# Score stage: a compare of broadcast column rows in place of turned one-hots, and byte addresses in the step tables

## The reference

```python
k, q, v = typed_linear(x, ntype, Wk/Wq/Wv)      # 8 heads of 16
kT = einsum('nhd,htdo->nhto', k, Watt)          # for each of 32 edge types
vT = einsum('nhd,htdo->nhto', v, Wmsg)
a = einsum('ehd,ehd->eh', kT[src, :, etype], q[dst]) * pri / SQRT_D   # the scores
att = edge_softmax(a, dst)
hag = segment_sum(vT[src, :, etype] * att, dst)
```

## Time and profile before

| what | value |
|---|---|
| time, median of 3 runs | 6493.91 us (6492.32 to 6510.61) |
| time of the profiled execution | 6516.86 us |
| its span, first to last instruction | 6515.1 us |
| busy: PE, PEld, DVE, ACT, POOL | 3454.9, 2426.0, 2199.7, 1126.3, 3210.2 us |
| granted TensorE clock, mean | 0.658 |

### The profile page before, as it was taken

One profiled execution on the slowest core, in us unless ns is written; L12 is line 12 of the kernel. 1 busy time (PEld: TensorE's weight loads), 2 busy tenths in 40 slices (PEclk: granted clock), 3 DMA queues, 4 the chain that ended last, 5 costly groups with the idle time before them and its releaser, 6 DMA issues. The chain is left out here.

```text
span 6515.1 us, 60996 instructions
## 1 busy us (share of the span) xinstructions
PE 3454.9 (53%) x14685; PEld 2426.0 (37%) x14685; DVE 2199.7 (34%) x5075; ACT 1126.3 (17%) x2416; POOL 3210.2 (49%) x3406
## 2 busy tenths in 40 slices
PE   5555777767774555633453336644435266444353
PEld 3333545445552333332333322244335222333353
DVE  3222222322224223311121114433348444333485
ACT  0000222222222111100000002310105233011053
POOL 4665566556654665466556651066540410655403
PEclk7666777676676666655665557755558677555586
DMA  2111334333432332311131128944434489444343
GB/s 60 47 47 37 92 100 100 88 90 96 100 94 83 91 91 67 109 47 47 59 115 47 46 61 335 395 129 130 127 97 141 122 347 386 127 128 127 96 140 99
DMA packets 600939, 772.17 MB, mean 119 GB/s; under 512 B 89734, under 2 KB 507000, under 8 KB 588064
## 3 DMA queue, kind: packets, MB, share of 16 engines
q1 hardware_dynamic: 480000, 492.16, 22.6%
q0 software_dynamic: 120608, 276.12, 16.2%
HBM read 416.10 MB, written 351.82 MB: 118 GB/s over the span
## 5 line engine op out<-in xcount | busy, mean ns | idle before, releaser
L453 POOL DMA_INDIRECT arena<-table,idx_s x3128 | 2989.8, 956 | 2458.4 <-issue 995.9
L735 PE MATMUL ps<-arena,work 128*128 x4160 | 968.1, 370 | 953.0 <-issue 884.8
L735 PEld LDWEIGHTS ps<-arena,work 128*128 128x128 f32 x4160 | 815.3, 269 | 1207.8 <-issue 1207.4
L1917 PE MATMUL ps<-ident,onehot 128*128 128x128 f32 x832 | 217.7, 413 | 671.5 <-DVE onehot L429 543.5
L433 DVE TENSOR_SCALAR work<-iota_row,dl_s,w_s 128x128 f32<-128x128 f32 x1248 | 351.6, 361 | 456.7 <-issue 316.1
L429 DVE TENSOR_TENSOR work<-ps,dl_s 128x512 f32<-128x512 f32 x208 | 143.9, 692 | 934.1 <-issue 612.4
L1877 DVE TENSOR_TENSOR arena<-arena,ps 128x128 f32<-128x128 f32 x832 | 183.9, 283 | 806.5 <-POOLq L449 382.5
L1917 PEld LDWEIGHTS ps<-ident,onehot 128*128 128x128 f32 x832 | 142.2, 207 | 728.8 <-DVE onehot L429 588.4
L909 DVE SCALAR_TENSOR_TENSOR arena<-ps,vecs,arena 128x256 f32<-128x256 f32 x208 | 100.7, 484 | 896.2 <-ACT arena L888 440.9
L1928 PE MATMUL ps<-arena 128*128 x1664 | 391.4, 413 | 5.1 <-issue 3.6
L1928 PEld LDWEIGHTS ps<-arena 128*128 128x128 f32 x1664 | 352.7, 313 | 26.5 <-issue 17.1
(11 more groups left out here) (329 smaller groups left out, 4139.0 us busy)
## 6 DMA issues: line engine op xcount, KB each, us to landing
table<-arena SPq DMA_DIRECT2D x96, 2048.0 KB
values<-arena SPq DMA_DIRECT2D x832, 64.0 KB
arena<-values SPq DMA_DIRECT2D x208, 256.0 KB
arena<-table,idx_s POOLq DMA_INDIRECT x3128
arena<-edge_times SPq DMA_DIRECT2D x208, 128.0 KB
edge_part<-arena SPq DMA_DIRECT2D x208, 128.0 KB
table<-arena SPq DMA_DIRECT2D x50, 512.0 KB
arena<-edge_part SPq DMA_DIRECT2D x98, 256.0 KB
```

The lines of the kernel that those rows point to most:

```text
L453: pool.indirect_dma_start(ring[:, ds(t % RING * 2 * H, width)], None, tab, bass.IndirectOffsetOnAxis(ap=idx_s[:, t:t + 1], axis=0)).then_i ...
L735: mm = pe.matmul(accf[:, ds(b, P)], o, ring[:, ds(slot, H)], start=False, stop=False, skip_group_check=True)
L1917: mm = pe.transpose(ps[:, q % 2, c * P:(c + 1) * P], onehot[:, 4 * q + c, :], ident[:, :])
```

## The change

The score stage no longer turns one-hots. Once, in the first layer's table stage, TensorE turns `dl_s` into 104 rows of 512 numbers, one row to a quad, ScalarE copies them out and SP stores them to device memory (`col_rows`). In the score stage ScalarE's queue starts, for each quad, a transfer that broadcasts that row over all 128 partitions (256 KB). VectorE compares it with the partition's own number (`node_no`) in one TENSOR_SCALAR of 128x512, and has the one-hot with nodes on partitions at once (`across`). It runs 7 quads ahead of the multiply. ScalarE computes nothing there any more. `rest` of the score stage's gathers goes from 2 to 4. In all passes `slot_i` and `blk_i` now hold byte addresses, which an engine loads into a register and uses as they are. The core of the diff:

```diff
-        def step_blocks(pe, j, n=U):
-            pe.load(first_cols[0:n], blk_i[0:1, ds(j, n)])
-            return [pe.snap(r, min_val=0, max_val=(NB - 1) * P) for r in first_cols[0:n]]
+        def addresses(eng, source, base, first, top):
+            regs = [eng.alloc_register(f"at_{next(loads)}") for c in range(source.shape[1])]
+            eng.load(regs, source)
+            return regs, [eng.snap(r, donate=True, min_val=base + 4 * first, max_val=base + 4 * top, guaranteed_mod_val=0, out_of_modulus=4) - base
+                          for r in regs]
+        def step_blocks(pe, j, n=U):
+            regs, places = addresses(pe, blk_i[0:1, j:j + n], PSUM_AT, 0, (NB - 1) * P)
+            return regs, [v // 4 for v in places]
...
-                        gathers(pool, table32, 2 * H, freed, rest=2)
+                        gathers(pool, table32, 2 * H, freed, rest=4)
...
+                    @block.scalar
+                    def _(act):
+                        for n in range(ALL_QUADS):
+                            if n >= QUADS:
+                                act.wait_ge(onehot_ready.sem, onehot_ready.at(n - QUADS + 1))
+                            act.dma_start(cols_ring[:, n % QUADS, :], col_rows[n, :].partition_broadcast(P)).then_inc(row_in[n % QUADS].sem, 16)
...
+                        def across(n):
+                            dve.wait_ge(row_in[n % QUADS].sem, row_in[n % QUADS].at(16 * (n // QUADS + 1)))
+                            if n >= DEEP:
+                                dve.wait_ge(made.sem, made.at(n - DEEP + 1))
+                            dve.tensor_scalar(across_ring[:, n % DEEP, :], cols_ring[:, n % QUADS, :], node_no[:, 0:1], None,
+                                              ALU.is_equal).then_inc(onehot_ready.sem, 1)
...
+                        for n in range(AHEAD):
+                            across(n)
+                        for n in range(ALL_QUADS):
+                            if n + AHEAD < ALL_QUADS:
+                                across(n + AHEAD)
+                            multiply(n)
+                            if n > 0:
+                                reduce(n - 1)
...
-                        def turn(i, q, fresh):
...
-                                mm = pe.transpose(ps[:, q % 2, c * P:(c + 1) * P], onehot[:, 4 * q + c, :], ident[:, :])
...
+                            for c, b in enumerate(blocks[n % QUADS * 4:n % QUADS * 4 + 4]):
+                                mm = pe.matmul(ps[:, n % 8, c * P:(c + 1) * P], across_ring[:, n % DEEP, c * P:(c + 1) * P],
+                                               Qn_flat[:, ds(b, P)], start=True, stop=True)
```

More of the change, by code:

```diff
@@ L53 @@
 DEEP = 12
+PSUM_AT = 1 << 25
 RELUS = 10
@@ L1680, in _ @@
                     def _(pe):
-                        regs = (first_cols + slot_cols + sum_cols)[0:SORT_TILES]
+                        regs = [pe.alloc_register(f"at_{next(loads)}") for n in range(SORT_TILES)]
                         for t in range(0, SORT_TILES, U):
@@ L1872, in multiply @@
+                        def multiply(n):
+                            slot_regs, slots = step_slots(dve, n * 4, 4)
                             dve.wait_ge(arrived.sem, step_need(dve, n) + arrived.base)
                             dve.wait_ge(made.sem, made.at(n + 1))
-                            if not (first and q < 2):
+                            if n >= 2:
                                 dve.wait_ge(copied.sem, copied.at(n - 1))
                             for c in range(4):
-                                product = dve.tensor_tensor(prod[:, q % 2, c, :], ring[:, ds(slots[c], H)], ps[:, 4 + q, c * P:(c + 1) * P], ALU.mult)
+                                product = dve.tensor_tensor(prod[:, n % 2, c, :], arena[:, ds(slots[c], H)], ps[:, n % 8, c * P:(c + 1) * P], ALU.mult)
@@ L1886, in lagged @@
-                        def lagged(i, q, first):
-                            if not (first and q < 2):
-                                multiply(i if q >= 2 else i - 1, (q - 2) % QUADS, first)
-                            if not (first and q < 3):
-                                reduce(i if q >= 3 else i - 1, (q - 3) % QUADS)
-                        onehots(dve, None, lagged, iota=ps[:, 2, 0:P])
-                        for q in range(QUADS - 2, QUADS):
-                            multiply(TRIPS - 1, q, False)
-                            reduce(TRIPS - 1, q - 1)
@@ L1896, in _ @@
-                        reduce(TRIPS - 1, QUADS - 1)
-                    @block.scalar
-                    def _(act):
-                        def body(i, first):
-                            for q in range(QUADS):
-                                n = i * QUADS + q
-                                act.wait_ge(quad_done.sem, quad_done.at(n + 1))
-                                if not (first and q < 2):
-                                    act.wait_ge(made.sem, made.at(n - 1))
-                                act.activation(onehotT[:, q % 2, :], ps[:, q % 2, :], ACT.Copy).then_inc(evac.sem, 1)
-                        trips(act, body)
+                            dve.tensor_reduce(score[:, 4 * n:4 * n + 4, :].rearrange("p s h -> p (s h)"),
+                                              prod[:, n % 2, :, :].rearrange("p s (h o) -> p (s h) o", o=HS), AX.X, ALU.add).then_inc(copied.sem, 1)
@@ L1945, in score_phase @@
+                for s in row_in:
+                    s.base += 16 * TRIPS
+                for s in (mixed, made, copied):
                     s.base += ALL_QUADS
```

159 lines of the change are left out of this document (92 added, 67 removed).

## The result

The changed kernel takes 6419.42 us (median of 4 runs, 6405.30 to 6431.97), the kernel before beside it 6499.83 (4 runs, 6492.32 to 6510.61). The ratio is 0.9874, with a 95% interval of 0.9854 to 0.9894: 1.3% or 80 us faster, where 127.5 were forecast. The time is inside the range.

The account below looks back on a forecast made before the run. GpSimd's 391 gather starts and the idle time between them were taken to bound each pass. Terms -119.5 + 27 + 5 - 43 + 3 = -127.5 us made 6493.9 into 6366 us, range 6305 to 6440.

Parts of the forecast that it names:

- Fewer waits: Score stage: GpSimd's waits for its newest quad fall from 48 to 24 a pass, gaining 119.5 us.
- the terms behind it: Everything but the waits: compare +27, rows +5, TensorE's gain -43, one-off setup and table work +3 us.
- The compare: Score stage: VectorE's compare stretches GpSimd's gathers by 0.13 us a quad, 13.5 us a pass, 27 us in all.
- the four short ones of pass 0: Pass 0's four 128x128 TENSOR_SCALARs a quad left gathers no longer, giving the compare's lower bound of 0 us.
- The full lock: Rival, score stage: each compare locks GpSimd out for its whole length, 62 us a pass; 6464 or 6507 us; chance 0.10.
- The broadcast rows: Score stage: rows seldom land in front of a gather GpSimd waits for; 0.1 us a wait, 5 us in all.
- Turning removed: Score stage: dropping 104 x 4 transposes and 104 copies a pass gains nothing, as TensorE and ScalarE waited anyway.
- Byte addresses: Passes 0, 4, 5 and their tails: 23% fewer TensorE sequencer instructions gain 43 us, of 64 at most.
- the rival on slow stepping: Passes 0, 4, 5: TensorE's long idleness before matmuls with no event to wait for stays; 6409 us; chance 0.20.
- the first rival: Same as the rival on slow stepping: only the score stage gains, -84.5 us, 6409 us; chance 0.20.

Follow-up runs that it names:

- e2: The kernel before with only the score stage's `rest` changed from 2 to 4: 6307.16 us, ratio 0.9809.
- e5: The changed kernel as it is, run again in a later set: 6352.74 us, ratio 0.9880 to the kernel before.
- e3: The changed kernel with only the first 4 quads' rows moved in each pass and never replaced: 6311.22 us, ratio 0.9817 to the kernel before.
- e8: The changed kernel with a second compare, to a tile nobody reads, for 97 of 104 quads of a score pass: 6383.68 us, ratio 0.9929 to the kernel before.
- e1: The changed kernel with the score stage's `rest` put back from 4 to 2: 6523.41 us, ratio 1.0145 to the kernel before.
- e4: The changed kernel with the score stage's `rest` raised from 4 to 8: 6266.71 us, ratio 0.9745 to the kernel before.
- e9: The kernel before with only the score stage's `rest` changed from 2 to 8: 6243.58 us, ratio 0.9711.
- e6: The kernel before with byte addresses in all passes and score stage `rest` 4, one-hots still turned: 6312.93 us, ratio 0.9816.
- e12: The changed kernel with `rest` 8 in all gather passes: 6008.03 us, ratio 0.9346 to the kernel before.
- e7: The changed kernel with broadcast rows in bfloat16, half the size (128 KB): 6341.67 us, ratio 0.9866 to the kernel before.

## Why the prediction was right, and where it was off

**Fewer waits: right.** -119.5 us forecast, 124 measured alone (e2). It is the whole gain. All else in the change costs 45.6 us together (e5 against e2), which the terms behind it had as -8.

**The compare: sign right, three to six times too large.** 27 us forecast, 4 measured in e3 with all the small edits, and some 2 to 4 us a pass by GpSimd's busy time. The lower bound, read from the four short ones of pass 0, was the nearer row, and the middle between rows wasn't justified. The full lock didn't show: 373.59 us, not 430. What set the price was where a compare begins, which the forecast didn't ask (e8).

The Trainium skill (SBUF — State Buffer, Who interferes with whom) has the one that issues first keep the shared pair for its whole instruction while the other is blocked. The traces agree in part: the 1.90 us operation of the earlier trace rows held a gather up for 1.5 us, compares begun just ahead of a gather held it up by 0.1 to 0.2 us on average, and compares begun 0.45 to 0.7 us into one took 0.1 us longer themselves. They do not agree where a compare begins in a gather's first 0.4 us: neither waits. The same section of the Trainium skill has an operation with two inputs in SBUF contend with a GpSimd instruction that reads SBUF. A gather reads its indices, `idx_s`, from there, so the 1.49 us of the earlier trace rows fits the page; the prediction called it a contradiction.

**The broadcast rows: the step that failed most.** I wrote: "Most landings fall elsewhere: I take 0.1 us a wait, 5 us." The runs show 0.7 us a wait and 34 us in all in the first comparison, and 0.9 us a wait and 42 us in all in e5 against e3, close to the upper bound of "a whole row each time, 0.9 us x 48 waits = 43 us". The mistake was to treat the start of a row and GpSimd's wait as independent. The row waits for a compare, the compare for the multiply, the multiply for the hand-over, and the hand-over is what comes just before the wait. That the waits lengthen with rows in flight is shown (e1, e3, e4 with e9), and within the traces that the moment decides: 3.84 us where the row starts early, 2.80 where it starts late or not at all; in e5 4.33 for 21 early ones and 3.19 for the other 27, less cleanly divided. No run moved the rows on purpose. That it is by packets in front of the gather's on the transfer engines is what the timeline suggests, and not shown.

**Turning removed: right.** It was forecast at nothing, and gave nothing: e3, which has no turning and no traffic of rows, is no faster than e2.

**Byte addresses: mechanism unproved, size wrong.** -43 us forecast. In the first comparison passes 0, 4 and 5 gained 3.6 us and their tails 2.5 + 6.3 + 7.3 = 16.1, some 20 in all, read from one trace of each kernel; that the edit made them isn't shown. The stalls stayed, and that is what the rival on slow stepping said. Without slow stepping the edit is worth nothing (e6). Too many instructions, on which my term rested, can't be its cause alone: e5 has the same ones as after and e2 those of before, and neither steps slowly. Where it comes from stays open. Between the first comparison and e5 the changed kernel became 67 us faster by the medians and 51 by the profiled executions, of which 36.5 are in these three passes and 7.6 in pass 0's tail. It affected both kernels nearly alike, so that the ratio is the same with it and without it, 0.9874 and 0.9880.

The Trainium skill (Runtime: NRT & Kernel Launch, Instruction fetch mechanics) has the cost of fetching mostly hidden. That fits e5, where 0.5 us is left by issue, and would not fit the 294.8 us of after if that idleness were a fetch, which no run shows.

**Sum.** In the profiled executions: -80.9 in the score passes, some -20 by TensorE's passes, and -6 in small differences elsewhere, -107; forecast -127.5. The total, 80 us, lies nearer to the 84.5 of the first rival than to the forecast. That rival was right that slow stepping stays. The second, the full lock, was wrong in its size. Inside the score stage, rows that cost about 30 us more than their 5 and compares that cost about 20 less than their 27 cancelled for the most part: -80.9 for -87.5 is luck, not a sum that was right term by term. Of the signs that I named, the waits are 3.5 us and not 2.7, GpSimd's busy time 373.59 and not 383, the compare 0.519 and not 0.48, passes 4 and 5 559.0 and 552.4 us and not 543, their tails 11.3 and not 13.

## What to carry to other kernels

On the engine that bounds, look first for the waits for its own newest transfer, and count them: here each cost 2.5 us above the plain gap after every 8 x 1.25 = 10 us of gathers, and letting the engine run ahead of them in all passes was worth 9.6%, while taking work off engines that wait anyway was worth nothing.

Before a new transfer is called hidden, follow what starts it. If what starts it hangs on an event just ahead of the bounding engine's wait, they meet most times (33 of 48 here), and the price lies near the upper bound and is not a small share of it.

Before two engines' operations are said to disturb each other, look at where one begins in the other, and not at their lengths alone.

When one change holds several edits, run the smallest of them alone: the changed `rest` alone gave 124 us, and the whole change 76.

## What the runs showed of the hardware

- A wait for the newest indirect gather was 2.75 to 2.88 us with rows of 1 KB for each index (before, e2) and 2.4 us with rows of 512 B (pass 5 of e2), with the plain gap of 0.30 in it. With broadcast rows of 256 KB on the same transfer engines it averaged 3.5 to 3.8 us in a pass (after, e1, e5; in e12, with 12 waits in a pass, 4.3 and 3.3), with rows of 128 KB 0.2 us less than in e5 (e7).
- The lengthening goes by the moment: 3.84 us where the broadcast starts from 0.5 us before to 0.95 us after the gather's start, 2.80 us where it starts from 1.23 us after it or not at all (after).
- A VectorE compare of 128x512 in SBUF takes 0.48 us alone and 0.58 to 0.59 us when it begins 0.45 to 0.7 us into a gather; a gather takes 0.95 us alone and 1.04 to 1.16 us when a compare begins 0.05 to 0.35 us ahead of it (after, e5, e8).
- The same program showed TensorE idle by issue for 294.8 us of a pass in one set of runs and for 0.5 us in another.
- The gathers' own pace, 0.95 + 0.30 us, didn't change between a share of the transfer engines of 0.18 and one of 0.66.
